# The product of the states with C on GpSimd in operations of 512 columns in place of 256, with new orders of turns

## The reference

```python
for i in range(NUM_LAYERS):            # 4 layers
    x = mamba_block(layer_norm(x, ln_w[i], ln_b[i]), ...) + x
# inside a block: 256 channels (d), 16 states (s) for each, 256 steps of time
dA = jnp.exp(dt_t[:, :, None] * A)
h = dA * h + dt_t[:, :, None] * B_t[:, None, :] * u_t[:, :, None]
y = jnp.einsum('bds,bs->bd', h, C_t)
...
y = (y + u * Dp) * jax.nn.silu(z);  out = y @ Wo.T
```

## Time and profile before

| | |
|---|---|
| median of 3 runs | 1874.89 us (1874.24 to 1879.85) |
| the profiled execution | 1869.66 us, its span 1867.8 us |
| busy: PE, DVE | 1482.4 us, 1481.1 us (79% each) |
| busy: ACT, POOL | 1339.2 us (72%), 1325.9 us (71%) |
| the groups on DVE | L1049 584.4 us, L1041 347.5 us |
| the product with C on POOL | L1060 906.7 us, 1024 operations |
| from the first recurrence to the last | 110.3 us to 1641.6 us |

### The profile page before, as it was taken

The page is one execution under the profiler, slowest core; times in us unless marked ns, Lnnn a source line. Parts: engine busy times, 40 slices in busy tenths (PEclk is TensorE's granted clock), DMA queues, the critical chain, the costliest instruction groups (busy, mean ns, idle before and its releaser), DMA issues.

```text
span 1867.8 us, 28242 instructions
## 1 busy us (share of the span) xinstructions
PE 1482.4 (79%) x9417; PEld 1056.2 (57%) x9417; DVE 1481.1 (79%) x2326; ACT 1339.2 (72%) x2730; POOL 1325.9 (71%) x1767
## 2 busy tenths in 40 slices
PE   6677766666899988567878999778889986889975
PEld 2443433334677666434455777556667664667854
DVE  6588898899999899978987978887988998721254
ACT  4476656666998787767687878788887886654453
POOL 3158678777788789887766867799978897830046
PEclk7676776787999999787788999989999998989997
DMA  5033222433544334220334444332545433212300
GB/s 192 1 75 73 63 66 69 109 82 96 134 119 116 120 108 108 69 59 23 91 102 108 130 126 138 86 107 56 132 137 132 132 96 69 66 43 74 124 6 6
DMA packets 84591, 170.15 MB, mean 91 GB/s; under 512 B 9440, under 2 KB 14944, under 8 KB 84064
## 3 DMA queue, kind: packets, MB, share of 16 engines
q1 hardware_dynamic: 84448, 168.37, 32.9%
HBM read 99.12 MB, written 2.10 MB: 54 GB/s over the span
## 4 chain that ended last, share of the span: by engine, by line
PE 23%; DVE 14%; ACT 9%; POOL 7%; issue 3%; DMA 2%; SPq 0%; DVEq 0%; POOLq 0%; ACTq 0%
DVE m L1049 5%; DVE dtuB L1041 3%; POOL m L1060 3%; PE ps L1467 3%; ACT m L1025 3%; PE ps L1475 2%; PE ps L1314 2%; PE ps L1758 2%; PE ps L1182 2%; PE ps L1080 2%; PE ps L964 2%; POOL o L1660 1%; PE ps L1325 1%; POOL o L1655 1%; ACT L347 1%
## 5 line engine op out<-in xcount | busy, mean ns | idle before, releaser
L1060 POOL TENSOR_TENSOR m<-m 128x256 f32<-128x256 f32 x1024 | 906.7, 920 | 92.5 <-DVE m L1049 84.9
L1049 DVE TENSOR_TENSOR_SCAN m<-m,dtuB 128x1024 f32<-128x1024 f32 x256 | 584.4, 2283 | 32.8 <-PE ps L1080 9.6
L1025 ACT ACTIVATE m<-m,Aneg 128x255 f32<-128x255 f32 x1024 | 429.8, 497 | 24.3 <-DMA m<-m 17.0
L1041 DVE TENSOR_TENSOR dtuB<-m 128x1024 f32<-128x1024 f32 x256 | 347.5, 1357 | 14.0 <-DMA m<-spread 5.2
L1467 PE MATMUL ps<-o 128*128 128x256 f32 x512 | 149.0, 402 | 18.9 <-DVE X L1411 7.1
L1080 PE MATMUL ps<-m,w_const 128*32 128x256 f32 x2048 | 151.5, 426 | 10.2 <-POOL m L1060 10.2
L1434 ACT ACTIVATE o<-ps,w_mo 128x256 f32<-128x256 f32 x256 | 113.4, 470 | 60.1 <-PE ps L1467 58.6
L364 POOL TENSOR_TENSOR o<-o,mhalf 128x2 f32<-128x2 f32 x64 | 19.4, 304 | 170.2 <-DVE o L358 170.2
L1182 PE MATMUL ps<-o 128*128 128x256 f32 x512 | 125.8, 395 | 13.2 <-ACT o L1151 8.2
L964 PE MATMUL ps<-m,wc 128*128 128x256 f32 x512 | 134.4, 421 | 2.0 <-ACT m L385 2.0
L1475 PE MATMUL ps<-o 128*128 128x128 f32 x1024 | 128.8, 279 | 5.5 <-ACT o L1434 4.8
(11 more groups left out here) (251 smaller groups left out, 2909.7 us busy)
## 6 DMA issues: line engine op xcount, KB each, us to landing
m<-m SPq DMA_DIRECT2D x256, 256.0 KB, 4.8
m<-spread SPq DMA_DIRECT2D x64, 512.0 KB, 5.4
o<-in_mox SPq DMA_DIRECT2D x128, 256.0 KB, 3.1
o<-in_l1x SPq DMA_DIRECT2D x88, 256.0 KB, 3.1
w_mb<-in_mb SPq DMA_DIRECT2D x1, 2288.0 KB, 11.8
m<-in_cwr SPq DMA_DIRECT2D x1, 2048.0 KB, 15.6
w_l3f<-in_l3f SPq DMA_DIRECT2D x1, 1536.0 KB, 17.6
X<-in_x SPq DMA_DIRECT2D x4, 256.0 KB, 6.6
```

The costliest lines, as they stand in the source:

```text
L1025: op = e.activation(dA[at % NA][:, j, 1:CH], R[q][:, h * CH + 1:h * CH + CH], ACT.Exp, scale=Aneg[:, l, 4 * g + j:4 * g + j + 1])
L1041: e.tensor_tensor(dtuB[:, :, :], bc(R[q][:, (2 + h) * CH:(3 + h) * CH].unsqueeze(1), 4, CH), Br[k % 2], ALU.mult).then_inc(S.dve, n.tick(f ...
L1049: e.tensor_tensor_scan(flat(G[at % NG]), flat(dA[at % NA]), flat(dtuB[:, :, :]), 0.0, ALU.mult, ALU.add).then_inc(S.dve, n.tick(f"s{g}"))
L1060: op = e.tensor_tensor(part, part, Cr[k % 2][:, j:j + 1, :], ALU.mult)
```

## The change

POOL's product takes two of the four states in one operation, so a group is two operations of 512 columns in place of four of 256. The columns, the data and the semaphore behind the last operation are as before. Beside it all five strings of ORDER are written anew, with the same number of turns of each kind on each engine. The first line of the string for `dve` and the last line of that for `pool` stand for them.

```diff
     "dve":
-        "aua7u4bub7a11bafabfb3aba5bab4fb2fs3fsbsbs6bsb2sb2fs10fsf2s5as3a2f2a2fasfs4as4asba2sas2a2fs3baba3sfbabfbfa2s6bs5b2"
+        "au2a7u2bu2b7a11ba2fb2fb3a4ba3b4fb2sfs2fsbs2bs4bs2b2sb2fs8fs2f2as8a2sfa2fasf2s6as3a3safsbasas3b2a4sfbabfba2fs10bs"
...
     "pool":
...
-        "s3bsa4faba4bas3a10sb2ab7sbs4b9abs2ba2b3a4b4a10b10a4b2ab2ab3ab2a2ba",
+        "asafasbs3ba4faba4bas3a10sb3absb6s4b9abs2ba2b3a4b4a10b10a8b4ab2ab4",
...
                     e.wait_ge(S.dve, n.dve(f"s{g}"))
-                    for j in range(0, 4, 1):
-                        part = G[at % NG][:, j:j + 1, :]
-                        op = e.tensor_tensor(part, part, Cr[k % 2][:, j:j + 1, :], ALU.mult)
+                    for j in range(0, 4, 2):
+                        part = G[at % NG][:, j:j + 2, :]
+                        op = e.tensor_tensor(part, part, Cr[k % 2][:, j:j + 2, :], ALU.mult)
                     op.then_inc(S.pool, n.tick(f"c{g}"))
```

More of the change, by code:

```diff
@@ L217 @@
[L217 to L221, removed]
@@ L236 @@
-    "act":
[L237 to L248, removed]
@@ new lines @@
+        "ba3ba2b5a2b2a4b3ab3abab2a2bab2",
+    "dve":
+        "au2a7u2bu2b7a11ba2fb2fb3a4ba3b4fb2sfs2fsbs2bs4bs2b2sb2fs8fs2f2as8a2sfa2fasf2s6as3a3safsbasas3b2a4sfbabfba2fs10bs"
+        "b3sbfs8fs2fafs8a2sb2fafa2b2fb2sbfb2s10afs10fs2f2s9a2f2afasfs2bfs13b2fa2fbfbsbfsasfbasab2absbs6bfbs7a2bfsf2s2a2sa"
+        "b2asbs4fs10fs2f2as2a2sbsbs2asbsafsb2abs3fsaf2s3as8fsabs3fbabf2s2abs4as4abafs2abas2bas2a2fsbf2s3as2bs7a2fa3bfa2f2"
+        "as3bs2as3bas2asb2sasa4baba2fabs2aba2bs4a2sfs2f2s2a7fb6sb3s2bsbsfbs4b8abs2fba2fb2fa2fab2s3absbs2bsb2sb2asfs4asafa"
+        "f2s4a2s6as2a2sabsfb2sbsbfbs2f2s6bs2bsb3a2sfb2s6afba2f2absb2s8fs6asfa2f2s4ab2as4b2asbsfbas4as5fas2f2sasbsb2as2bs2"
+        "afbsa2s2bsfa2f2bas2a2sbs3bs3fba3sa5bas4basab2fasf2sfsb2a8basb2a2s2as2fsa2s2b3asasas2ab3sfb2f2bs3fsbab2as4b4sb2a3"
+        "s2ab3s2fb2sbs2bsbfsf2s2bsbs3abs3a2bfs4as2fs2f2sas4bsbs2as3fbfbabf2s3bs2as8fsas5fbf2s2ab2s2bs2bs4afs2bs2as2bfsf2s"
+        "bs6bs4a2fbsbasfas2baf2sasas2b2s3a3bsa3ba2fabs2b2a3s4a8bab2sabfbasbasfsa2b3s2a2ba2b2s5b6sb3s2abab2sba2fa2fb5a4b2a2"
+        "b4a2bab2abab2ab2a2b2a2baba2b5a3b2a6b3a2b3ab3a2ba2b2a5b6ab3a2b3ab",
@@ new lines @@
+    "act":
+        "a3ua4ua2ua2bua2ba2ba5b2ab2ab5ab2a2b6a3bafabf2abfbfbfafa2b3asa2sbfbsba2sfa2fs3af2af2b2sababsabsas2basb2sf2sasbf4b"
+        "asb2sfbsasfasbfabfbfsfba3s3ba3s2ba3fasa2fabas2bf2bf2as2a3sa2s2a3s2fafs3fbf2b2fab3s2absf2s2af2bfsfb2s2bs2b3sb4s3b"
+        "fbfs2af2bf2sb2fs4f2sasaf3sbfaba2s2abfbabfafas3a2fb2fa2fsbfs2abasba2bs3a2fa2fa2babfabfsfasfas2ab2asasasb2asasab3a"
+        "fbfs2afabfbsfb2afaba3b2asab2asabsasa2baf2sbs2bfbfsfbfaba3bsa4bs2a3bafbafasasasfafabafsafb4a2s2b4absbab2sba2sasb2"
+        "abfsfsafabfsf2b3absb3sa2fbasfb3s3fb3a2fbsafsab2afba2sba4sb2sabsbsa2bfbsa2fbafsa2fb2fafsafab3a2ba2ba3basasb2asb2a"
+        "bfbafabfbsbs2f3asfb4sb4sb2s2b2a2fafsb3s2abafafsfa2bafbsa2ba2sbs3f2s2bfba2fafasfb3a2sba3bsbas2baf2ab2afafsafs2afa"
+        "b2sas2ab2asas2ab2abf2bas2afabfba2fb2afa2b2sabasab2a2basabsabasbsaba2bsa2bfabfs2a2bafafbafbsa2fba4b2sb2sbasab2sba"
+        "fb2fb2asfbabafb2safbab2fba2bab3s2b4sa2b3aba2sb2fas2af2asbf2abfasfa3sbab2abasa2bababs2a2s2a2bafaba2fbfb2sbfabfa2b"
+        "a2sfsa2safab3a3b2asbas2babsbafbafs2fbfbafsfsb2a2b2s3ababs2bfabfs2asaf2babfa2fa2b4sba2saf2sb2s2fabafsfba2fsb2sb2s"
+        "ba2bs2abaf2as2ab2a2fbfsfsbfb3sba4b2sbs2b4sa2bf2bs2b2fbafsfb3afsb4a2sb4asb2sasb2fa2fsas2bafabfafafbsa2ba2babasaba"
+        "bsbababs2a4sa2b2a4b3a2bsa2bsba4b2sb2ababa7bababab2a2ba2b2ab2ab2a2b2a3b2a2b4a2ba2b4a2b2a2b3a2ba2ba4b2a4b5a3b3abab4"
+        "a3b4ab3ab5ab4ab4a2babababa2b4a3b3a3bab3ab3a2b3aba2bab2",
```

38 lines of the change are left out of this document (17 added, 21 removed).

## The result

The kernel after takes 1869.46 us, median of 20 runs (1861.74 to 1878.03); the kernel before, measured beside it 20 times, 1875.4 us (1865.72 to 1882.44). The ratio is 0.997 with a 95% interval of 0.9956 to 0.9983: faster by 0.3%, some 6 us. The forecast was 3 us the other way, 1878 us. The profiled execution of after took 1864.92 us, with a span of 1863.1, 4.7 us under that of before, at a mean granted clock of 0.878 (before 0.876).

A forecast was written before the change was run, and what follows sets the result against it. No engine was full; DVE, 90% busy in places, POOL beside it and the chain of waits bounded the kernel. Terms -8 + 9 + 0 + 2 + 0 = +3 us gave 1878 us; 8-in-10 range 1858 to 1896.

The forecast's parts named there:

- The product's own cost: POOL's L1060: two 512-column operations take 2.50 us a group against 2.78, saving 72 us over 256 groups.
- What the longer operation does to DVE: DVE's L1041 and smaller operations wait longer behind POOL's products: the loss grows from 50 to 79 us, +29 us.
- the working by half a product: A DVE operation arriving at random in POOL's products waits half of one: 0.36 us before, 0.63 us after.
- The price of that time: Of DVE's +29 us, 30% counts, L1041's share of the chain of waits: +9 us, bounds 0 and +50.
- The price of POOL's time: Of the product's 72 us saved on POOL, 11% counts, its share of the chain: -8 us, bounds 0 and -21.
- the slower rival of the prediction: DVE's longer waits decide, at L1041 where DVE is 88% to 90% busy: +25 us for the wait, 1894 us; chance 0.29.
- The order in between: Turns between start and end move by a few places on the engines: 0, with 10 us on either side.
- The start and the end: Start: DVE's +2.9 us against PE's -1.0 and -1.9, sum 0; end: o1's second half of L3Ffn later on DVE, +2 us.
- the waits named as signs: Waits of ACT and PE for other engines should move if shares or new order were misjudged by over 10 us.

## Why the prediction was wrong, step by step

**The product's own cost: right.** Forecast were a median of 1.27 us and a sum of 835 us; measured 1.272 and 825.0. L893 was the row to go by.

**What the longer operation does to DVE: right in kind, somewhat too high.** Forecast was +29 us of DVE time and a mean of L1041 of at least 1.43; measured were +27.7 with the old orders (mean 1.421) and +22.7 with the new (1.409). Its greatest, 2.38 us, is the least 1.20 and 1.18 more, nearly one product of 1.27. The rule of the Trainium skill ("SBUF — State Buffer", section "SBUF: two separate sides"), by which the ports are locked for the whole instruction, agrees with that and with the 3.43 us beside 1024 columns. But the working by half a product, which I took from it, fails for short ones: beside 256 columns the greatest L1041, 2.10 us, has 0.90 more than its least, longer than a product of 0.73, and beside 128 columns one of 4.02 us stood while eight products went by.

**The price of that time, "By L1041's share of the chain 30% counts: +9": wrong.** With the orders of before it is near 100%: 23 us for 27.7, 18 to 21 for 19.2, 63 for 68.4. With the new ones it is about 45% for the memset of 192 columns, still above 30%. The chain of waits says which instruction ended last at each step; it doesn't say that the other 70% could take more without anything moving. My reading, which no run tests by itself, is that in an order that is written out a later L1041 delays all that stands behind it on DVE, whether or not the chain passes through L1041. The 90% busy of the earlier trace rows was the better guide here: DVE had hardly any room in the old order.

**The price of POOL's time, "11% counts: -8": too high with the old orders, the other way round from DVE's.** With the old orders 178 us less on POOL gave 11 us, all of which DVE's own 15 us less explain. Both errors made the operation alone look cheaper than it is, +1 us forecast and +23 measured; the slower rival of the prediction (+25 for the wait) is what the old orders show. With the new orders the product costs +1 us, within 5, and +1 was the forecast for it. That agreement is luck: it comes from an order in which both prices differ from the one that the shares were read from.

**"The order in between: 0": wrong, and the step that turned the sign.** This term was put at nothing because no row gave it a sign. The new orders alone bring -7 us, within the 10 us on either side that I gave; with -7 in place of 0 the sum is -4, and -6 was measured. But the prediction added the terms, and these two don't add: with the new orders the longer product costs 1 us or so (0.07% by the ratios, intervals of 0.13% and 0.21% either way) in place of 23. Put together, the orders are worth 7 us for the short product and 29 us for the long one. I had looked for a sign of the new order in waits and had not asked whether it changes the price of the other part.

**The start and the end.** L416 began at 15.31 us (forecast 14.8), yet the first recurrence came at 107.36 us, 2.9 before that of before, forecast 0. From the last recurrence to the end it took 222.4 us against 226.2, -3.8, forecast +2. Each is one execution of each kernel. Counted at the first recurrence of a unit, after is ahead by 9.7 us at unit 12, 13.0 at unit 23, 1.0 at unit 26, 1.0 at the end of the scans and 4.7 at the end of the program. So the 12 us are lost between units 23 and 26, which take 175.9 us in after and 163.8 in before, at a clock of 0.89 against 0.93. The orders alone lose 7 us in the same three units. The low clock of 0.83 from 1500 to 1650 us, against 0.91 in the earlier trace rows, lies behind that and goes with no further loss.

**What stays open.** Shown is that the new orders give 7 us by themselves, that the longer product costs 23 us with the old orders and about nothing with the new ones, and that other time on DVE costs about half of what it did. Whether POOL's relief counts more with the new orders, where in the program the saving lies, and which of the moved turns make room is not settled: the waits that I compared give no single place. Strings of some engines taken from before and of others from after were not tried.

Of the waits named as signs, two moved: L838's wait for PE fell from 26.6 to 7.8 us, and L374's for the norm on POOL from 39.8 to 33.3. The new orders do it, not the product (9.2 and 34.3 with the orders alone, 25.6 and 38.6 with the operation alone). These are rows of after, total, times and longest:

```profile
ACT o L374 <- POOL o L369: 33.3, 28, 4.4
...
DVE m L838 <- PE ps L1080: 7.8, 9, 2.2
```

## What to carry to other kernels

The share that a line has on the chain of waits is not the price of a microsecond more on it: on an engine that runs a fixed list at 90% busy, count up to all of it, and give a saving and an addition on its neighbour different prices. Where a change brings an operation and a new order together, try each alone and both: the order was worth four times as much with one form of the operation as with the other, which no sum of terms shows. A longer operation on GpSimd is to be judged by what it locks on VectorE as well as by its own time.

## What the runs showed of the hardware

- The product on POOL of two SBUF tiles takes, by medians, 0.452 us for 128 columns, 0.726 for 256, 1.272 for 512; the least for 1024 is 2.341. Worked out from these, that is about 2.1 ns a column and 0.18 us for each operation.
- POOL and DVE hold each other up. Beside products of 256, 512 and 1024 columns L1041's greatest is 2.10, 2.38 and 3.43 us, and with 1024 columns the product's median is its least and most of an L1041. Beside products of 128 columns one L1041 took 4.02 us while eight of them went by: the wait can be longer than one operation of the other engine.
- A memset of 64 columns ahead of L1041 on DVE (0.11 us) adds nothing to the period of a group, one of 192 columns (0.22 us) adds 0.13 us (3.86 in place of 3.73).
